# A row gather with a bound on its indices: leaving out skip edges in the last stage of a graph network kernel

## The reference, cut to what matters

```python
h = (x_flat @ W_gat).reshape(M, HEADS, NUM_EXPERTS)          # M = 6250, 4 heads, 4 experts
e = leaky_relu(a_src[src] + a_dst[dst], negative_slope=0.2)
ee = jnp.exp(e - e_max[dst])
denom = jax.ops.segment_sum(ee, dst, num_segments=M)
msg = h[src] * (ee / (denom[dst] + 1e-16))[:, :, None]
agg = jax.ops.segment_sum(msg, dst, num_segments=M) + b_gat   # then norm, top 2 of 4, softmax: the gates
out = out + g[..., None] * (gelu(x @ W1[ei] + b1[ei]) @ W2[ei] + b2[ei])
```

## Time and profile before

| | us |
|---|---|
| median of 3 runs | 4448.03 |
| lowest, highest | 4445.95, 4449.41 |
| the profiled execution's own time | 4443.94 |
| its span | 4442.2 |
| busy in the span: PE, DVE, POOL, ACT | 3555.7, 3146.5, 2791.1, 2405.8 |

### The profile page before, as it was taken

One profiled execution on the slowest core, in us unless ns is written; L12 is line 12 of the kernel. 1 busy time (PEld: TensorE's weight loads), 2 busy tenths in 40 slices (PEclk: granted clock), 3 DMA queues, 4 the chain that ended last, 5 costly groups with the idle time before them and its releaser, 6 DMA issues. The chain is left out here.

```text
span 4442.2 us, 67327 instructions
## 1 busy us (share of the span) xinstructions
PE 3555.7 (80%) x17780; PEld 2268.9 (51%) x17780; DVE 3146.5 (71%) x10069; ACT 2405.8 (54%) x5553; POOL 2791.1 (63%) x2880
## 2 busy tenths in 40 slices
PE   6698999999999998788878778854377777777773
PEld 5555566666666665444444445443144444444442
DVE  7776666565656664788888888875667777777777
ACT  7343323333233332599999964434466666666664
POOL 0274677576665400477777777754777777777775
PEclk9998999999999999899999999965689899898986
DMA  3333222121221101655555556534222222222221
GB/s 102 82 89 113 44 40 46 32 46 33 44 44 29 28 1 37 185 140 143 145 143 144 144 151 162 158 89 109 34 40 40 40 40 39 40 40 40 39 39 28
DMA packets 290605, 331.30 MB, mean 75 GB/s; under 512 B 79040, under 2 KB 244929, under 8 KB 290233
## 3 DMA queue, kind: packets, MB, share of 16 engines
q0 software_dynamic: 105328, 175.77, 19.3%
q1 hardware_dynamic: 184904, 151.23, 12.3%
HBM read 289.56 MB, written 30.77 MB: 72 GB/s over the span
## 5 line engine op out<-in xcount | busy, mean ns | idle before, releaser
L3186 POOL DMA_INDIRECT st_rows<-tabr,router_rsrc x1072 | 1030.6, 961 | 329.8 <-issue 318.5
L2516 POOL DMA_INDIRECT all_XT<-tab,graph_gsrc x880 | 843.7, 959 | 272.6 <-issue 232.1
L1476 POOL DMA_INDIRECT st_rows<-tab,graph_gsrc x748 | 733.3, 980 | 384.4 <-issue 203.6
L1731 ACT ACTIVATE st_h<-st_ph,st_shift,st_scale 128x448 f32<-128x448 f32 x448 | 324.4, 724 | 744.7 <-PE st_ph L1592 744.4
L2546 PE MATMUL st_po<-all_XT,st_hot 128*128 128x264 f32 x1760 | 517.5, 441 | 105.5 <-DVE gat_sum L2756 102.4
L3243 PE MATMUL st_py<-st_w,st_hid 128*128 128x256 f32 x1568 | 441.2, 430 | 2.4 <-ACT st_hid L3291 2.4
L2756 DVE TENSOR_TENSOR gat_sum<-gat_sum,st_po 128x264 f32 x880 | 375.7, 427 | 71.2 <-PE st_po L2546 2.3
L2546 PEld LDWEIGHTS st_po<-all_XT,st_hot 128*128 128x128 f32 x1760 | 299.1, 202 | 248.3 <-issue 112.8
L3231 PE MATMUL st_px<-all_XT,st_w 128*128 128x512 f32 (+2 forms) x832 | 396.6, 624 | 15.1 <-ACT st_hid L3291 15.1
L3205 PE MATMUL st_pad<-st_adr,st_hott 128*128 x1072 | 68.1, 175 | 399.4 <-DVE st_zd L3357 386.3
L1605 PE MATMUL st_po<-all_XT,st_h 128*128 128x256 f32 x1568 | 371.9, 386 | 8.5 <-DVE all_X L1922 6.7
(11 more groups left out here) (546 smaller groups left out, 7291.8 us busy)
## 6 DMA issues: line engine op xcount, KB each, us to landing
st_bc<-drowr SPq DMA_DIRECT2D x268, 128.0 KB
st_bc<-drow SPq DMA_DIRECT2D x220, 128.0 KB
st_rows<-tabr,router_rsrc POOLq DMA_INDIRECT x1072
all_XT<-tab,graph_gsrc POOLq DMA_INDIRECT x880
st_xtb<-xtd SPq DMA_DIRECT2D x98, 128.0 KB
st_rows<-tab,graph_gsrc POOLq DMA_INDIRECT x748
xtd<-all_XT SPq DMA_DIRECT2D x49, 128.0 KB, 1.7
all_XT<-xtd SPq DMA_DIRECT2D x49, 128.0 KB
```

The source lines that it names most:

```text
L1476: g.indirect_dma_start(self.rows[:, b, u, :], None, self.R.tab0, bass.IndirectOffsetOnAxis(self.R.gsrc[:, t:t + 1], 0)).then_inc(self.s_ro ...
L1731: a.activation((self.h1, self.h2)[l][:, fb, h * HALF:(h + 1) * HALF], self.ph[:, m % 3, 0:HALF], ACT.Relu, bias=self.shift[:, l, i:i + 1], ...
L2516: g.indirect_dma_start(self.rows[:, b, u, :], None, self.R.tab1, bass.IndirectOffsetOnAxis(self.R.gsrc[:, t:t + 1], 0)).then_inc(self.s_ro ...
L3186: g.indirect_dma_start(self.rows[:, b, u, :], None, self.R.tabr, bass.IndirectOffsetOnAxis(self.R.rsrc[:, t:t + 1], 0)).then_inc(self.s_ro ...
```

## The change

The split computes, for each edge, whether its relative destination is below 0 or above 127, and adds 16384 to the clamped source of such an edge. The gather of the last stage takes a bound of 6271 (`NP - 1`) on its indices. Since left-out rows keep what the ring holds, POOL zeroes the ring once at the start of the last stage and waits for that.

```diff
+SKIPPED = 1 << 14
...
+        self.s_out_of = f.sem("qoutof")
...
             v.wait_ge(self.s_cut, 2 * j + 2)
-            v.tensor_scalar(self.srcf[:, j], self.srci[:, j % 2], float(N - 1), None, ALU.min).then_inc(self.s_split, 1)
             v.tensor_scalar(self.dstf[:, j], self.dsti[:, j % 2], self.off[:, j:j + 1], None, ALU.subtract)\
+                .then_inc(self.s_split, 1)
+            far = self.dsti[:, j % 2].bitcast(F32)
+            v.wait_ge(self.s_split, 2 * j + 1)
+            v.tensor_scalar(far, self.dstf[:, j], 0.0, None, ALU.is_lt).then_inc(self.s_out_of, 1)
+            v.wait_ge(self.s_out_of, 3 * j + 1)
+            v.scalar_tensor_tensor(far, self.dstf[:, j], float(P - 1), far, ALU.is_gt, ALU.add).then_inc(self.s_out_of, 1)
+            v.tensor_scalar(self.srcf[:, j], self.srci[:, j % 2], float(N - 1), None, ALU.min).then_inc(self.s_out_of, 1)
+            v.wait_ge(self.s_out_of, 3 * j + 3)
+            v.scalar_tensor_tensor(self.srcf[:, j], far, float(SKIPPED), self.srcf[:, j], ALU.mult, ALU.add)\
                 .then_inc(self.s_split, 1)
...
-        self.s_far, self.s_col = f.sem("far"), f.sem("col")
+        self.s_far, self.s_col, self.s_clean = f.sem("far"), f.sem("col"), f.sem("clean")
...
     def pool(self, g):
+        g.memset(self.rows[:, :, :, :], 0.0).then_inc(self.s_clean, 1)
+        g.wait_ge(self.s_clean, 1)
         for q in range(self.GROUPS):
...
                 g.indirect_dma_start(self.rows[:, b, u, :], None, self.R.tabr,
-                                     bass.IndirectOffsetOnAxis(self.R.rsrc[:, t:t + 1], 0)).then_inc(self.s_rows[b], 16)
+                                     bass.IndirectOffsetOnAxis(self.R.rsrc[:, t:t + 1], 0), bounds_check=NP - 1,
+                                     oob_is_err=False).then_inc(self.s_rows[b], 16)
```

## The result

The changed kernel takes 4509.88 us (median of 3 runs, 4506.78 to 4513.08) against 4448.03: a ratio of 1.0134, 95% interval 1.0119 to 1.0148. It is 62 us slower. The forecast's own case, 4456, did not come; what came is the mechanism of rival two, near the half price that it named.

The account below looks back on a forecast made before the run. POOL's row gathers were taken to pace the last stage, with DVE not far behind. Split 7.2 + memset 0.8 + bound 0 = 8.0 us, taking 4448.0 to 4456.0; own range 4448 to 4459, wide range 4395 to 4515.

Parts of the forecast that it names:

- The forecast's own case: Whole kernel: the split and the memset add 8.0 us, the bound nothing, so the median becomes 4456.0 us.
- rival two: Last stage's gather: the bound costs POOL time on every gather, hidden by nothing; 4458 to 4561 us; chance 0.28.
- half price: Last stage's gather: the bound costs half of a 98 ns POOL pass per gather, 52.5 us more, 4509 us.
- main case: Last stage: gather time unchanged by the bound, total 4448.8 to 4458 us; chance 0.41.
- last sign: Gathers changing by more than a few ns at the median would make the prediction wrong, whatever the split costs.
- What bounds the kernel: Last stage: POOL sets the pace with 1072 gathers, about 1.25 us each, filling 1360 us; DVE not far behind.
- The split, 7.2 us: Table stage on DVE: rounds grow from 0.73 to 1.66 us, making PE's third turn 7.2 us late.
- The memset, 0.8 us: Start of the last stage: POOL zeroes the ring and waits, delaying the first gather by 0.8 us.
- The bound at 0: Last stage's gather: the bound adds 0 us, since gathers with other row sizes also take 944 to 946 ns.
- Rival two's doubt: Last stage: gathers that waited for DVE lost only the usual 0.30 us gap, so a small addition could vanish.
- Rival one: Last stage: skipped rows are cheaper on POOL, up to 40.9 us before 4100 and 17.0 after; 4408 us; chance 0.31.
- Rival three: Last stage's gather: rows are fetched anyway or skipped rows cost as much; 4456 us; chance counted with the forecast.

## Why the prediction was right or wrong

- **The number: 4456 missed, the range held.** The measured 4510 lies within 4395 to 4515 only because the range was drawn over half of rival two, to which 0.28 was given against 0.41 for the main case. By the prediction's own last sign, gathers that change by more than a few ns, its main case was wrong.
- **What bounds the kernel: right.** POOL paces the last stage; 52.5 us more busy time there became 52.2 us more from first to last gather, and with the bound alone 50.0 us more busy time made the kernel 50.6 us slower.
- **The split, 7.2 us: right in size and place.** The round is 1.64 us (forecast 1.66), PE's wait stands at the third turn, and the run with the split alone gives 6 to 14 us. The stage is 7.0 us longer in two of the four profiles with this split and 8.7 in the other two, where PE's clock falls once more behind the third turn; of the clock the prediction says nothing.
- **The memset, 0.8 us: right.** From the end of the reduction ahead of it (3058.60 + 0.39) to the first gather pass 4.24 us; in the trace of before 3.39 us. That is 0.85 us. No run has the memset alone.
- **The bound at 0: this step failed.** I took the value that the gathers of the trace repeat, 944 to 946 ns whatever they fetch. But no gather there had a bound, so the rows had no say on its price. It is 53 ns a gather at the median, 47 on the mean, 50.6 us in the run with the bound alone: nearly all of the 54 us by which the forecast case of 4456 was too low. Nor do all gathers of that trace take 944 to 946 ns: seven in the front stage (L691) took 977 to 2161 ns, which the prediction passes over and no run explains. Rival two, that every gather pays and nothing hides it, is what happened. That its half price gives 4509, within 1 us of the run, is luck: 49 ns are half the price of a 128x1 memset, and nothing ties the bound to a memset.
- **Rival two's doubt** (a small addition beside the instruction can vanish) was right for the move, 29 ns, which cost nothing, and wrong for the bound, which is inside the instruction.
- **Rival one: its tail was right, its premise wrong.** Taking away the gathers behind slot 832 gives 15.3 us where it said 17.0. But a gather's 944 ns are not 7.4 ns a row: 0.9 ns a row by the run with fewer rows, and left-out rows save not even that. The Trainium skill, page "DMA: Bandwidth & Descriptors", section "SWDGE vs HWDGE vs iDMA", has one descriptor pair computed for each DMA operation. No run here shows that work by itself; all that goes with the rows is 0.9 of 7.4 ns each, and a left-out row still goes through the queue, as the last section shows.
- **Rival three** is half out: the bound does something, since the gather queue moves 172.97 MB instead of 175.77. But its second form, that a skipped row costs POOL as much as a fetched one, is what the runs show; only the price of the bound was missing from it.

## What to carry to other kernels

An instruction's option has a price of its own, and rows of the instruction without it cannot bound that price at zero; where an engine goes from one such instruction to the next without a pause, some 50 ns times 1072 are most of the result. Ask what an indirect gather's time hangs on before thinning it out: here some 0.83 of 0.94 us are per gather, so half the rows save 45 ns and rows left out by a bound nothing. Fewer gathers save more, but only as far as the other engines allow: 15 us when the last 240 went alone, 276 when their work on DVE, PE and ACT went with them. And an idle time that equals the engine's usual gap between two instructions is no slack.

## What the runs showed of the hardware that I had not expected

**A left-out row is not nothing.** The gather queue has 105,328 packets in both kernels. 36,899 rows of 80 bytes are left out (288.27 slots of 128), 2.95 MB, but only 175.77 - 172.97 = 2.80 MB are missing: 76 bytes a row. By the trace's records it is exact: 175,769,600 - 172,965,276 bytes = 36,899 x 76, so 4 bytes remain for each row. 4,373 packets have 32 bytes, eight times 4, where all packets of this gather had 640, eight rows. So a left-out row still goes through the queue as a small transfer, which fits that it saves POOL no time; where the 4 bytes go the trace does not tell. So "nothing is to be copied" is not quite what happens: 76 of a row's 80 bytes are not moved, 4 are.

**PE's clock dips where the split holds PE back.** Three stretches of the table stage of the changed kernel (busy PE, PEld, DVE, ACT, POOL, then granted clock, DMA share, GB/s), then the middle one in the kernel before; below them, from the second profile of the changed kernel, PE's third and fifth turn and the stretch between them:

```profile
1800.00:1812.00 12.00, 8.76 (x43) 6.75 (x44) 11.30 (x40) 5.84 (x25) 0.00 (x0) 0.96 0.47 160
1812.00:1820.00 8.00, 6.59 (x21) 4.90 (x21) 7.45 (x32) 2.15 (x8) 0.00 (x0) 0.64 0.55 186
1820.00:1830.00 10.00, 9.61 (x56) 8.02 (x57) 5.16 (x21) 5.22 (x19) 0.00 (x0) 1.00 0.41 138
...
1812.00:1820.00 8.00, 7.61 (x45) 6.26 (x44) 3.55 (x14) 4.50 (x18) 0.00 (x0) 1.00 0.51 169
...
1815.44 0.30 PE L2188 MATMUL tab_qpt<-all_ident,all_XT 128*128 128x128 f32 x1 [3.15 <-DVE tab_qdst_rel L2163]
...
1819.86 0.27 PE L2188 MATMUL tab_qpt<-all_ident,all_XT 128*128 128x128 f32 x1
...
1815.40:1820.00 4.60, 4.56 (x18) 3.61 (x19) 2.49 (x10) 1.23 (x4) 0.00 (x0) 0.63 0.16 54
```

The granted clock is 0.64 on the mean between 1812 and 1820, a mix of the two levels (1.2 and 2.4 GHz), after PE had idled 2.2 us up to 1809.6, since the late normalisations began only at 1809.1; in the kernel before it is 1.00 there. In this execution the dip lies ahead of the third turn, where PE waits 1.41 us for the copy all the same, so it adds nothing to the 7.0 us that the trace shows. In the second profile PE waits 3.15 us for that copy, and behind the third turn the clock falls again, to 0.63 on the mean. From the third turn to the fifth 4.4 us pass there instead of 2.7, and that 1.7 us is what makes the stage 8.7 us longer instead of 7.0; the run with the bound in a register shows the same. Whether a second dip follows differs from execution to execution; what decides it no run shows.
